# A four-layer graph network: b1 added while the hidden tile leaves PSUM, the norm's weight on GpSimd, the root used as a scale

## The reference

```python
neighbor_sum = jnp.einsum('bnm,bmd->bnd', adjacency, x)
agg = epsilon * x + neighbor_sum
h = jnp.einsum('bnd,dh->bnh', agg, W1) + b1          # 256 -> 1024
h = jax.nn.silu(_rmsnorm(h, rms_weight))             # h * rsqrt(mean(h^2) + eps) * w
out = jnp.einsum('bnh,hd->bnd', h, W2) + b2          # 1024 -> 256
```

## Time and profile before

| | us |
|---|---|
| median of 3 runs | 3686.64 (3686.24 to 3687.06) |
| profiled execution | 3683.56 |
| its span | 3681.6 |
| TensorE busy | 3536.5 (96%) |
| VectorE busy | 2646.7 (72%) |
| ScalarE busy | 2288.2 (62%) |
| GpSimd busy | 772.0 (21%) |

### The profile page before, as it was taken

The page is one execution under the profiler, slowest core; times in us unless marked ns, Lnnn a source line. Parts: engine busy times, 40 slices in busy tenths (PEclk is TensorE's granted clock), DMA queues, the critical chain, the costliest instruction groups (busy, mean ns, idle before and its releaser), DMA issues.

```text
span 3681.6 us, 68425 instructions
## 1 busy us (share of the span) xinstructions
PE 3536.5 (96%) x19886; PEld 2496.9 (68%) x20108; DVE 2646.7 (72%) x6474; ACT 2288.2 (62%) x5062; POOL 772.0 (21%) x1611
## 2 busy tenths in 40 slices
PE   6999999999999999999999999999999999999997
PEld 4666667666677666676666776666776666766664
DVE  5777777777777777777777777777777777777764
ACT  3666566665676665666656766656666656666564
POOL 1122221222221222212222212222112222122210
PEclk8999999999999999999999999999999999999999
DMA  2232222232232332232322323322323222223212
GB/s 88 58 92 79 70 76 73 70 92 69 69 86 52 92 85 70 68 80 63 92 69 70 85 56 87 89 72 63 90 53 92 76 70 78 70 73 92 69 53 63
DMA packets 166940, 275.09 MB, mean 75 GB/s; under 512 B 23908, under 2 KB 59876, under 8 KB 166760
## 3 DMA queue, kind: packets, MB, share of 16 engines
q1 hardware_dynamic: 166760, 273.45, 27.9%
HBM read 122.37 MB, written 16.78 MB: 38 GB/s over the span
## 4 chain that ended last, share of the span: by engine, by line
PE 52%; issue 14%; DVE 14%; ACT 9%; POOL 6%; DMA 2%; SPq 2%; POOLq 0%; DVEq 0%; ACTq 0%; another core or an unknown queue 0%
PE turn L1259 8%; PE value L1274 7%; PE front L1066 6%; PE score L1249 5%; PE front L1067 5%; PE front L1068 5%; PE score L1250 3%; PE front L1096 3%; ACT pT L615 3%; POOL small L398 3%; DVE pT L845 3%; POOL x_out L464 2%; DMA qk_stack<-qk 2%; ACT prob L606 2%; PE front L1108 2%
## 5 line engine op out<-in xcount | busy, mean ns | idle before, releaser
L606 ACT ACTIVATE prob<-prob,small 128x512 f32<-128x512 f32 x1024 | 736.0, 719 | 398.8 <-DVE small L921 397.1
L921 DVE CUSTOM_DVE_ANT_0 prob<-score,adj_sb,drv 128x512 f32<-128x512 f32 x1024 | 760.0, 747 | 150.3 <-PE score L1250 89.0
L1259 PE MATMUL turn<-ident,prob 128*128 128x128 f32 x4096 | 614.9, 275 | 15.3 <-ACT pT L615 8.2
L1259 PEld LDWEIGHTS turn<-ident,prob 128*128 128x128 f32 x4096 | 485.2, 141 | 114.7 <-issue 27.9
L615 ACT ACTIVATE pT<-turn 128x512 f32<-128x512 f32 x768 | 447.3, 585 | 112.3 <-PE turn L1259 112.2
L1249 PE MATMUL score<-qk_stack 128*128 128x512 f32 x1024 | 493.6, 486 | 24.4 <-DMA qk_stack<-qk 12.3
L1066 PE MATMUL front<-w_hi,s_hi 128*128 128x256 f32 x1024 | 356.2, 348 | 12.1 <-DVE drv L746 7.3
L1250 PE MATMUL score<-unlinked,neg_mask 128*128 128x512 bf16 x802 | 313.3, 391 | 0.0
L705 DVE TENSOR_TENSOR s_lo<-front,s_hi 128x512 fp32r<-128x512 f32 x320 | 219.5, 686 | 129.1 <-ACT s_hi L510 129.1
L1067 PE MATMUL front<-w_lo,s_hi 128*128 128x256 f32 x1024 | 289.6, 283 | 0.0
L1068 PE MATMUL front<-w_hi,s_lo 128*128 128x256 f32 x1024 | 289.0, 282 | 0.0
(11 more groups left out here) (182 smaller groups left out, 7787.6 us busy)
## 6 DMA issues: line engine op xcount, KB each, us to landing
qk_stack<-qk SPq DMA_DIRECT2D x1024, 128.0 KB, 2.4
adjT_f<-in_adjT SPq DMA_DIRECT2D x32, 1024.0 KB, 5.3
adj_sb<-in_adj SPq DMA_DIRECT2D x32, 1024.0 KB, 7.4
prob<-in_adjT SPq DMA_DIRECT2D x32, 1024.0 KB, 5.3
x_new<-in_x SPq DMA_DIRECT2D x32, 512.0 KB, 4.0
out<-x_out SPq DMA_DIRECT2D x32, 512.0 KB, 3.0
pT<-in_W SPq DMA_DIRECT2D x2, 1024.0 KB, 11.4
rmsw_b<-in_rmsw SPq DMA_DIRECT2D x1, 512.0 KB
```

What stands on the lines that cost most here:

```text
L606: act.activation(prob[:, i % 8, :], prob[:, i % 8, :], ACT.Exp, bias=nmax[:, h, n:n + 1], scale=-1.0, accum_out=prsum[:, h, n:n + 1]).then ...
L921: dve.tensor_tensor_reduce(out=prob[:, i % 8, :], in0=SB_[i % 2][:, :], in1=adj_sb[:, n, :], scale=neg_w[:, h:h + 1], scalar=3e38, op0=ALU ...
L1259: last = pe.transpose(TB[k % 2][:, tile(n)], prob[:, (4 * h + n) % 8, tile(j)], ident[:, :])
```

## The change

- b1 is no longer a product. It lies broadcast over all partitions (`b1_b`, 128 x 1024), and VectorE's new `hidden(tf, n, c)` adds it while it moves PSUM to `hid`, at u = 1, 2 (tile 0: before the loop, between the flags of missing edges and the degrees, which have become `sums`).
- ScalarE squares `hid` from SBUF and writes into the bank that VectorE has emptied. In the queue, square now comes behind the exponential of the step.
- GpSimd multiplies `hid` by the norm's weight (already times half the root of 1024), one half before and one behind its three small operations.
- tanh takes the root as its scale and writes into the PSUM bank; SiLU's product reads it there. The root is missing from `hid`, and `update0` multiplies by it. `aside` is gone; the saved diagonal has moved.
- In the first phase the hidden tiles of odd n use the score banks, and the preparation of the weights is spread over steps -4, 3, 11, 19 and 27 (ScalarE: 2 and 10). TensorE waits in step 6 for W2's low part alone, and for the rest behind the loop.

```diff
@@ sync
-            for r in range(4):
-                sp.dma_start(region[32 * r:32 * r + 1, 4096:4096 + N], b1[None, N * (r // 2):N * (r // 2) + N]).then_inc(w1_loaded, 16)
+            sp.dma_start(b1_b[:, :], b1[None, :].to_broadcast([P, F])).then_inc(w1_loaded, 16)
@@ gpsimd
             def hidden_norm(tf, n):
+                def weigh(c):
+                    cs = slice(N * c, N * c + N)
+                    pool.tensor_tensor(hid[:, cs], hid[:, cs], rmsw_b[:, cs], ALU.mult).then_inc(hid_ready, 1)
+
+                pool.wait_ge(squared, at(tf, 8, 2 * n + 1))
+                weigh(0)
                 pool.wait_ge(squared, at(tf, 8, 2 * n + 2))
...
                 pool.tensor_tensor(rms[:, n:n + 1], sse[:, n:n + 1], k_mhalf, ALU.pow).then_inc(rms_ready, 1)
+                weigh(1)
@@ scalar
             def square(tf, n, c):
-                act.wait_ge(hid_ps, at(tf, 8, 2 * n + c + 1))
...
-                act.activation(aside[:, :], FB[c][:, :], ACT.Square, accum_out=ss[:, n, c:c + 1]).then_inc(squared, 1)
+                act.wait_ge(raw_ready, at(tf, 8, 2 * n + c + 1))
...
+                act.activation(hidden_bank(tf, n, c)[:, :], hid[:, N * c:N * c + N], ACT.Square,
+                               accum_out=ss[:, n, c:c + 1]).then_inc(squared, 1)
             def tanh(tf, n, c):
...
-                act.activation(aside[:, :], hid[:, N * c:N * c + N], ACT.Tanh).then_inc(tanh_done, 1)
+                act.wait_ge(squared, at(tf, 8, 2 * n + c + 1))
+                act.wait_ge(rms_ready, at(tf, 4, n + 1))
+                act.activation(hidden_bank(tf, n, c)[:, :], hid[:, N * c:N * c + N], ACT.Tanh,
+                               scale=rms[:, n:n + 1]).then_inc(tanh_done, 1)
@@ scalar, the loop
                     if f:
                         for n, u in tile_steps(g):
-                            if n and u in (1, 2):
-                                square(tf, n, u - 1)
-                            elif u in (4, 5):
+                            if u in (4, 5):
                                 tanh(tf, n, u - 4)
...
                         exps(t, g + 4)
                     if b and g == -3:
                         values(t, 1)
+                    if f:
+                        for n, u in tile_steps(g):
+                            if n and u in (1, 2):
+                                square(tf, n, u - 1)
@@ vector
-            def hidden(tf, n):
-
-                dve.wait_ge(rms_ready, at(tf, 4, n + 1))
...
-                    dve.scalar_tensor_tensor(out=hid[:, cs], in0=FB[c][:, :], scalar=rms[:, n:n + 1], in1=rmsw_b[:, cs],
-                                             op0=ALU.mult, op1=ALU.mult).then_inc(hid_ready, 1)
+            def hidden(tf, n, c):
+
+                dve.wait_ge(hid_ps, at(tf, 8, 2 * n + c + 1))
...
+                dve.tensor_tensor(hid[:, cs], hidden_bank(tf, n, c)[:, :], b1_b[:, cs], ALU.add).then_inc(raw_ready, 1)
...
-                dve.tensor_tensor(x_in[:, n, :], down_bank(n), x_in[:, n, :], ALU.add).then_inc(x0_ready, 1)
+                dve.scalar_tensor_tensor(out=x_in[:, n, :], in0=down_bank(n), scalar=rms[:, n:n + 1], in1=x_in[:, n, :],
+                                         op0=ALU.mult, op1=ALU.add).then_inc(x0_ready, 1)
@@ vector, phases
                     graph(t)
+                if f:
+                    hidden(tf, 0, 0)
+                    hidden(tf, 0, 1)
+                if b:
+                    sums(t)
...
                         for n, u in tile_steps(g):
-                            if u == 3:
-                                hidden(tf, n)
+                            if n and u in (1, 2):
+                                hidden(tf, n, u - 1)
@@ tensor
-                pe.matmul(FB[c][:, :], ones_rows[:, c, :], b1_rows[:, :], start=True, stop=False)
...
-                    last = product(FB[c][:, :], (T_hi[:, k, tile(n)], T_lo[:, k, tile(n)]),
-                                   (w1_hi[:, k, cs], w1_lo[:, k, cs]), False, k == DT - 1)
+                    last = product(hidden_bank(tf, n, c)[:, :], (T_hi[:, k, tile(n)], T_lo[:, k, tile(n)]),
+                                   (w1_hi[:, k, cs], w1_lo[:, k, cs]), k == 0, k == DT - 1)
@@ tensor, phases
-                        pe.wait_ge(setup_dve, SETUP_DVE)
+                        pe.wait_ge(setup_dve, SETUP_W2)
...
+                if shared is not None:
+                    pe.wait_ge(setup_dve, SETUP_DVE)
                 if f:
                     turn(tf)
```

More of the change, by code:

```diff
@@ L223, in gnn_kernel, with hidden_bank @@
         Q1_STEP, K1_STEP = 0, 3
+        def hidden_bank(tf, n, c):
+            return (SB_ if isinstance(tf, int) and tf == 0 and n % 2 else FB)[c]
         def down_bank(n):
@@ L365, in _ @@
             sp.wait_ge(out_stored, 16 * B)
[L367 removed]
+        N_W1, N_W = 16 * 3, 16 * 11
         @block.gpsimd
@@ L497, in _ @@
             add_b2(0)
-            pool.wait_ge(setup_dve, 7)
+            pool.wait_ge(setup_dve, 1)
             phases(None, 0, 1)
@@ L625, in phases @@
                     qk_high(t, 0, 1)
-                if f:
-                    square(tf, 0, 0)
                 if b:
@@ L630, in phases @@
                 if f:
+                    square(tf, 0, 0)
                     square(tf, 0, 1)
                 for g in GRID:
+                    if g in prepare:
+                        prepare[g]()
                     if f:
                         for n, u in tile_steps(g):
-                            if n and u in (1, 2):
-                                square(tf, n, u - 1)
-                            elif u in (4, 5):
+                            if u in (4, 5):
                                 tanh(tf, n, u - 4)
@@ L705, in lo @@
                 return dve.tensor_tensor(dst, src, high.bitcast(F32), ALU.subtract)
[L707 to L710, removed]
             done(dve.memset(one_b, 1.0))
@@ L714, in prepare_w1 @@
                 dve.wait_ge(w1_loaded, N_W1)
[L715 to L719, removed]
                 done(dve.tensor_scalar(rmsw_b[:, :], rmsw_b[:, :], 0.5 * float(F) ** 0.5, None, ALU.mult))
@@ L723, in prepare_w1, with prepare_w2, prepare_low @@
                 assert step[0] == SETUP_W1, step[0]
-            def prepare_rest():
+            def prepare_w2():
+                dve.wait_ge(setup_act, 2)
+                done(lo(w2_lo[:, :, :], region[:, 2048:4096].rearrange("p (k n) -> p k n", k=FT), w2_hi[:, :, :]))
+                assert step[0] == SETUP_W2, step[0]
+            def prepare_low():
                 dve.wait_ge(setup_act, 5)
-                done(lo(w2_lo[:, :, :], region[:, 2048:4096].rearrange("p (k n) -> p k n", k=FT), w2_hi[:, :, :]))
                 done(lo(wl_lo[:, :, :], wl_stage, wl_hi[:, :, :]))
@@ L777, in diagonal @@
                 dve.wait_ge(adjT_f_loaded, at(tf, 16, 16))
-                if later(tf):
-                    dve.wait_ge(silu_ready, at(tf, 8, 0))
                 dve.tensor_copy(diag, diag_of(adjT_f)).then_inc(diag_saved, 1)
@@ L806, in silu @@
                 dve.wait_ge(tanh_done, at(tf, 8, 2 * n + c + 1))
-                dve.scalar_tensor_tensor(out=hid[:, cs], in0=aside[:, :], scalar=1.0, in1=hid[:, cs],
+                dve.scalar_tensor_tensor(out=hid[:, cs], in0=hidden_bank(tf, n, c)[:, :], scalar=1.0, in1=hid[:, cs],
                                          op0=ALU.add, op1=ALU.mult).then_inc(silu_ready, 1)
@@ L896, in graph, with sums @@
                 dve.tensor_scalar(unlinked[:, :, :], adj_sb[:, :, :], 0.0, None, ALU.is_equal).then_inc(unlinked_ready, 1)
+            def sums(t):
                 dve.tensor_reduce(deg, adj_sb[:, :, :], AX.X, ALU.add).then_inc(deg_ready, 1)
@@ L992, in phases @@
                                 stats(tf, 1, f_norm, norm_tiles(0), x_in, n)
-                    if prepare is not None and g == 3:
-                        prepare()
+                    if g in prepare:
+                        prepare[g]()
                     if b and g >= 0 and g % 4 == DVE_TURN:
@@ L1099, in hidden @@
             def hidden(tf, n, c):
-                if n:
+                if isinstance(tf, int) and tf == 0:
+                    if n > 1:
+                        pe.wait_ge(s_hi_ready, at(tf, 8, 2 * n + c - 3))
+                        pe.wait_ge(s_lo_ready, at(tf, 8, 2 * n + c - 3))
+                elif n:
                     pe.wait_ge(s_hi_ready, at(tf, 8, 2 * n + c - 1))
@@ L1118, in turn_hidden @@
                 for f in range(4):
-                    last = pe.transpose(FB[c][:, tile(f)], hid[:, tile(4 * c + f)], ident[:, :])
+                    last = pe.transpose(hidden_bank(tf, n, c)[:, tile(f)], hid[:, tile(4 * c + f)], ident[:, :])
                 last.then_inc(f_turned, 1)
```

61 lines of the change are left out of this document (28 added, 33 removed).

## The result

The changed kernel takes **3713.05 us** in the median (3712.28 to 3714.45, 4 runs) against 3686.44 of the kernel before beside it: a ratio of 1.0076, interval 1.0063 to 1.0088. It is 26.6 us slower. The forecast was 3701, so the side was right, the place in the batch was right, and the loss was 12 us larger than forecast. The profiled span went from 3681.6 to 3710.2 us.

A forecast was written before the change was run, and what follows sets the result against it. TensorE bounds, its helpers equally late in two places per batch; +0.66 us x 31 batches = +20.5, start -6, so 3683.56 + 20.5 - 6 = 3698 profiled, 3701 us as median; range 3660 to 3728.

The forecast's parts named there:

- transposition, step 8: Tile 1's transposition of a head's probabilities, awaiting its last exponential: starts at 37.83 instead of 1936.86, TensorE shifted +0.96 us.
- transposition, step 24: Tile 3's transposition of a head's probabilities, now at 1970.68: square between exponentials 26 and 27 adds 0.57, net +0.11.
- The two places with 0.06 us of room: Transpositions at 1936.86 and 1970.68: TensorE's queue done about 0.06 us earlier, so TensorE and the exponentials' chain equally late.
- turn waits ACT prob: TensorE's transposition of probabilities waiting for ScalarE's exponential: grows from 6.4 us to 55 to 65 us.
- Tile 0: Before the loop: additions delay first bias 0.56 us, second key product +0.2; the two products saved there bring nothing.
- Tile 1: Steps 4 to 8: addition +0.42 and square +0.57 delay the last exponential 0.98; 0.46 saved becomes a 1.3 us wait.
- Tiles 2 and 3: Steps 12 to 17 and 20 to 24: 0.46 us saved in each, net shifts +0.05 and +0.11.
- The rest of the period is TensorE's work and moves as a whole: Remainder of each batch's period adds no shift beyond the tiles' sum of +0.66 us per batch.
- The start: Batch 0's front alone: less waiting for prepared constants, -10 us into step 7, part returned; -6 taken, bounds 0 and -10.
- GpSimd: Eight multiplications of 512 columns per batch, 1.27 us each with no lock; bounds 1.26 and 1.71.
- the rival of 3740: GpSimd becomes the bound: under the lock each weighing takes 1.71 for 1.27, 41 us more at most; chance 0.08.
- TensorE busy some 60 us less: Sign of the forecast: TensorE's busy time falls some 60 us while its wait for the exponentials grows.

The follow-up runs named there:

- e5: Changed kernel with VectorE's degree sums moved from before the loop to the end of step 15, GpSimd's use to before tile 3's norm: 3700.10 us, 1.0041.
- e11: Changed kernel with VectorE's additions of b1 on one column instead of 512 in tiles 1 to 3 (times only): 3689.50 us, ratio 1.0015.
- e2: Changed kernel with the second half's square on one column instead of 512 in tiles 1 to 3 (times only): 3686.48 us, ratio 1.0009.
- e3: Changed kernel with GpSimd's multiplication by the norm's weight on one column of each half instead of 512 (times only): 3704.24 us, ratio 1.0055.
- e8: Changed kernel with tanh at scale 1.0 instead of the pointer to the norm's root (times only): 3702.41 us, ratio 1.0047.
- e4: Changed kernel with ScalarE writing the second keys' high part ahead of its step's exponential instead of behind exponential and copy: 3684.95 us, ratio 1.0004.
- e1: Kernel before without the product that puts b1 into PSUM, b1 left out (times only): 3653.67 us, ratio 0.9919.
- e9: Changed kernel with early second keys' high part and late degree sums, plus root before first weighing in the first front: 3673.86 us, ratio 0.9973.
- e10: Kernel before with ScalarE's early second keys' high part and the degree sums moved to step 15: 3732.67 us, ratio 1.0130.
- e7: Kernel before with ScalarE writing the second keys' high part ahead of its step's exponential: 3678.38 us, ratio 0.9985.

## Why the prediction was right, and what was too small

The sum was 20.5 for the batches and -6 for the start. Measured by the flags: 31.5 for the batches, -2.9 for start and end together. Shifts of TensorE within a batch, from the flags on, forecast and measured:

| place | forecast | measured | how |
|---|---|---|---|
| first bias | +0.56 | +0.49 | 1917.45 for 1916.96 |
| second key product, step 3 | +0.2 | +0.15 | 1926.24 for 1926.09 |
| bias 10 | +0.42 | +0.46 | 1934.39 for 1933.93 |
| transposition, step 8 | +0.96 | +1.06 | 1937.92 for 1936.86 |
| transposition, step 24 | +0.66 | +0.82 | 1971.50 for 1970.68 |
| whole period | +0.66 | +1.01 | 113.06 for 112.05 |

The same shifts against the kernel before in medians of 29 batches, for the changed kernel and for experiments that take one piece out:

| place | changed | e5, late sums | e11, addition | e2, square | e3, weighing | e8, pointer |
|---|---|---|---|---|---|---|
| tile 0's hidden transposition, second half | +0.04 | -0.44 | +0.03 | +0.03 | +0.03 | -0.20 |
| transposition, step 8 | +1.05 | +0.57 | +0.51 | +0.61 | +1.05 | +0.99 |
| before tile 2's hidden transposition | +0.53 | +0.06 | -0.01 | +0.08 | +0.53 | +0.38 |
| behind it | +0.69 | +0.22 | -0.01 | +0.24 | +0.53 | +0.44 |
| transposition, step 24 | +0.82 | +0.35 | +0.13 | -0.05 | +0.66 | +0.58 |
| transposition, step 28 | +0.97 | +0.50 | +0.27 | +0.09 | +0.81 | +0.54 |

- **What bounds the kernel, and where it is as late as its helpers**: right. The two places with 0.06 us of room are the two where the wait appeared, 1.28 (forecast 1.3) and 0.52 us (0.6), and "turn waits ACT prob" is 61.8 us against 55 to 65. e2, e4 and e11 show that the chain is the cause, and e1 that the saving is there without it.
- **Tile 0**: the shifts are right, and so is that the two products saved before the loop bring nothing: TensorE is 0.44 us early there, and the first score starts as before. But the late sums of e5 gain 0.43 per batch, more than the 0.15 that is left at step 3. I had not seen that the change could also bring SiLU's product of tile 0 forward, for which TensorE waits 0.41 us per batch in the kernel before, and that the late sums hold it at its old time.
- **Tile 1**: 0.10 too small. The square takes 0.62 from start to next start (1836.45 to 1837.07) where I took 0.57 from before, and the bias is 0.04 later.
- **Tiles 2 and 3**: 0.06 too small in sum. Tile 2's tanh starts at 1854.96 + 99.45 = 1954.41, as forecast (54.4), but TensorE loses 0.16 there and not 0.05. In e3, with the weighing cut short, it loses nothing there.
- **"The rest of the period is TensorE's work and moves as a whole"**: this step failed. Between step 24 and the period's end another 0.19 us is lost, 31 x 0.19 = 5.9 us, half of what the forecast missed. I priced tanh as unchanged and left ScalarE's pointer scale out. e8 has it at 0.38 per batch over all places, 0.24 of it ahead of step 24 and 0.14 behind. That leaves 0.05 of the 0.19 without a cause that a run shows. The nearness at step 24 is part luck: without the pointer the shift there is +0.58, so the forecast of +0.66, made without the pointer, was too high by what it priced.
- **The start**: 4 us too good. The first down product starts at 37.88 for 48.81, 11 us earlier, near my 39. But both squares of a tile come back to back there, and tanh waits 1.93 us for the weighing and the root (their order is without effect, e9). In e3 that is worth 4.3 us.
- **GpSimd**: right in its price, not in its being covered. The weighing takes 1262, 1286, 1307 ns (shortest, median, longest) against my 1.27 us, so no lock shows, and the rival of 3740 is out. But by e3 the weighing costs the 0.16 us of tile 2, 5 us over the batches.
- **TensorE busy some 60 us less**: 46.5. The neighbours take longer: the products of the two high parts, half of which now stand first in their bank, take 465 ns in the mean, where they took 398 behind the one with b1.

## What to carry to other kernels

Taking work off the busiest engine pays only where its helpers have room: look at how long TensorE's own queue had been done when the awaited operation ended, and if it is nearly nothing, price the helpers' chain, not TensorE's product. Then ask whether that chain follows TensorE or stands by itself: in e1 the saving was kept at step 24 and mostly lost at step 8. When a change puts an operation on a helper, look next for what stands in that helper's queue ahead of the chain and is not urgent: moving one ScalarE instruction gave back all that the change had cost. Price every operand that a change adds: a pointer scale of 90 ns cost 11 us. And whether a gap is free depends on the order around it: the same move of 2.28 us gained 13 us in one kernel and lost 54 in the other (e10 against e7).

## What the runs showed that was not expected

VectorE's tiny operations stretch beside GpSimd. In the first phase the signs of the constants (8 and 2 columns) run while GpSimd adds b2 from 24.99 to 27.76, and then weighs from 27.71 on; VectorE:

```profile
24.65 0.17 DVE L743 TENSOR_SCALAR drv<-drv 128x8 f32<-128x8 f32 x1
24.86 0.17 DVE L744 TENSOR_TENSOR drv<-cst,drv 128x8 f32<-128x8 f32 x1
25.06 0.68 DVE L745 TENSOR_SCALAR drv<-drv 128x8 f32<-128x8 f32 x1
25.77 0.65 DVE L742 TENSOR_SCALAR drv<-cst 128x2 f32<-128x2 f32 x1
26.45 0.65 DVE L743 TENSOR_SCALAR drv<-drv 128x2 f32<-128x2 f32 x1
...
27.81 1.19 DVE L745 TENSOR_SCALAR drv<-drv 128x2 f32<-128x2 f32 x1
```

0.17 us becomes 0.65 to 0.68 from the moment that GpSimd starts, each about one of its four additions (0.7 us) long, and 1.19 beside the weighing (1.26). The stretched ones shown have one SBUF input and a constant. The Trainium skill (SBUF — State Buffer, "Who interferes with whom") names tensor_scalar among the operations that can take the shared ports; this trace fits it. No run here prices it.

A square from SBUF into PSUM takes 587 ns in the mean, the one from PSUM into SBUF took 591. So no longer square appears where the prediction's estimate from the Trainium skill (VectorE: DVE Perf Modes, "The TRN2 errata") had 0.04 us for an SBUF source. That does not refute it, as the output moved as well: between the tanh of before and e8's, both from SBUF and without a pointer, the output in PSUM took 30 ns less (592 for 622). No run here moves the source alone.
